# Audio tower on one core: the second group norm of the token stage one iteration behind the first, and the heads' weight products in three 16-bit passes

## What is computed

```python
# token stage, for each of 16 images
h = conv1d(x, conv_in_w, pad=3)                      # 64 -> 128 channels, 7 taps, 2048 positions
h = gelu(groupnorm1(h, gn1_w, gn1_b))                # first norm
h = conv1d(h, dw_w, stride=2, pad=2, groups=H) + dw_b   # 5 taps, 1024 positions
h = gelu(groupnorm1(conv1d(h, pw_w), gn2_w, gn2_b))  # pointwise product, second norm
# attention stage, 32 heads, 128 tokens (channels) per image, width 1024
h = h + attention(layernorm(h))                      # latents of 384 and 128, rotary part of 64
# last stage: base product plus two of eight small experts
h = h + ffn(layernorm(h))
```

## Time and profile before

| | |
|---|---|
| median of 3 runs | 2040.95 us (2040.42 to 2043.39) |
| the profiled execution | 2044.69 us, its span 2042.9 us |
| TensorE busy | 1892.5 us, 93% of the span |
| VectorE busy | 1321.2 us, 65% |
| ScalarE busy | 773.2 us, 38% |
| GpSimd busy | 308.4 us, 15% |
| mean granted clock of TensorE | 0.969 of full |

### The profile page before, as it was taken

The page is one execution under the profiler, slowest core; times in us unless marked ns, Lnnn a source line. Parts: engine busy times, 40 slices in busy tenths (PEclk is TensorE's granted clock), DMA queues, the critical chain, the costliest instruction groups (busy, mean ns, idle before and its releaser), DMA issues. The chain is left out here.

```text
span 2042.9 us, 32412 instructions
## 1 busy us (share of the span) xinstructions
PE 1892.5 (93%) x11538; PEld 1029.6 (50%) x11538; DVE 1321.2 (65%) x2742; ACT 773.2 (38%) x2020; POOL 308.4 (15%) x596
## 2 busy tenths in 40 slices
PE   4898898559999999999999999999999999859999
PEld 2344444335555555555555555555555555425554
DVE  4678777436666666666666666666666666555554
ACT  3454554233333334433333433333343333332221
POOL 2376675300000000000000000000000000033332
PEclk9899999679999999999999999999999999979999
DMA  5244342332222322232222222223222222243332
GB/s 143 52 86 96 81 95 65 76 91 51 58 58 59 76 56 53 58 76 59 58 58 55 73 58 58 58 58 75 55 55 58 40 39 39 39 138 80 80 82 73
DMA packets 305609, 138.87 MB, mean 68 GB/s; under 512 B 295088, under 2 KB 295344, under 8 KB 303408
## 3 DMA queue, kind: packets, MB, share of 16 engines
q1 hardware_dynamic: 301136, 108.35, 24.8%
q10 hardware_dynamic: 4320, 28.51, 4.0%
HBM read 56.07 MB, written 8.39 MB: 32 GB/s over the span
## 5 line engine op out<-in xcount | busy, mean ns | idle before, releaser
L1031 PE MATMUL out_ps<-m_h,ot_h 128*128 128x512 f16 x1024 | 389.4, 380 | 1.7 <-DVE ot_l L835 1.7
L1032 PE MATMUL out_ps<-m_l,ot_h 128*128 128x512 f16 x1024 | 389.0, 380 | 0.0
L1033 PE MATMUL out_ps<-m_h,ot_l 128*128 128x512 f16 x1024 | 388.9, 380 | 0.0
L756 ACT ACTIVATE qp_h<-qp_ps 128x512 f16<-128x512 f32 x126 | 75.3, 597 | 492.6 <-PE qp_ps L966 492.6
L812 ACT ACTIVATE prob<-s_ps,nmx 128x128 f32<-128x128 f32 x512 | 181.3, 366 | 207.3 <-DVE nmx L905 207.3
L885 DVE SCALAR_TENSOR_TENSOR resid<-out_ps,resid 128x512 f32<-128x512 f32 x256 | 176.1, 688 | 97.1 <-PE out_ps L1033 97.1
L835 DVE SCALAR_TENSOR_TENSOR qp_l<-qp_ps,qp_h 128x512 f16<-128x512 f32 x126 | 87.2, 692 | 234.5 <-ACT qp_h L756 234.5
L1221 POOL MEMSET fpower<- 128x1 f32 x1 | 0.1, 99 | 1392.4 <-POOLq L674 1392.4
L966 PE MATMUL qp_ps<-lat,wp_h 128*128 128x512 f16 x756 | 205.6, 381 | 0.0
L1033 PEld LDWEIGHTS out_ps<-m_h,ot_l 128*128 128x128 f16 x1024 | 100.4, 98 | 121.6 <-issue 1.4
L1031 PEld LDWEIGHTS out_ps<-m_h,ot_h 128*128 128x128 f16 x1024 | 100.5, 98 | 110.5 <-DVE ot_l L835 2.7
(11 more groups left out here) (217 smaller groups left out, 3861.3 us busy)
## 6 DMA issues: line engine op xcount, KB each, us to landing
wide<-heads_in ACTq DMA_DIRECT2D x30, 928.0 KB, 4.7
wide<-x_in SPq DMA_DIRECT2D x30, 512.0 KB, 6.5
tower_out<-result SPq DMA_DIRECT2D x16, 512.0 KB, 2.6
stage<-wb_in SPq DMA_DIRECT2D x8, 512.0 KB, 8.3
resid<-wqk_in SPq DMA_DIRECT2D x1, 2304.0 KB, 11.6
zt<-z SPq DMA_TRANSPOSE x128, 2.4
turned<-halves SPq DMA_TRANSPOSE x128, 3.0
wide<-heads_in SPq DMA_DIRECT2D x2, 928.0 KB, 4.6
```

The lines of the kernel that those rows point to most:

```text
L756: act.activation(out, src, ACT.Copy, scale=scale).then_inc(done, 1)
L1031: pe.matmul(out_ps[hf][:, :], ot_h[:, h, :], m_h[:, at], start=h == 0, stop=False)
L1032: pe.matmul(out_ps[hf][:, :], ot_h[:, h, :], m_l[:, at], start=False, stop=False)
L1033: last = pe.matmul(out_ps[hf][:, :], ot_l[:, h, :], m_h[:, at], start=False, stop=h == HEADS - 1)
```

## The change

**Token stage.** HID, PROJ and TAIL come one iteration later (2, 3, 4 become 3, 4, 5); a step PW at lag 2 holds the pointwise product and its statistics, which were at the end of the iteration of the taps; LOW is folded into TAIL. The conv has two PSUM banks in place of three, the pointwise product two pairs in place of one, and the averages share the second bank of the conv. Tap 0 goes from VectorE to ScalarE. On each engine the order within an iteration is new. In the last iterations, without conv, `squares` moves behind the next image's `hid`.

**Attention stage.** The raw weights of heads 4 to 31 are split by ScalarE and VectorE into 16-bit halves, in three pieces, in slots 0 to 2 of a round, into the place of the second raw buffer. `split_products` makes each product of three 16-bit passes, one slot later than its piece. The next head is loaded in slot 3 in place of slot 0. The scales by which the products are split take account of the new factor.

```diff
-    AHEAD, MID, HID, PROJ, TAIL, LOW = -1, 1, 2, 3, 4, 5
+    AHEAD, MID, PW, HID, PROJ, TAIL = -1, 1, 2, 3, 4, 5
...
-        conv_ps = [pb("conv_ps0"), pb("conv_ps1"), pb("conv_ps2")]
-        stat_ps = pb("stat_ps")
-        pw_ps = [pb("pw_ps0"), pb("pw_ps1")]
+        conv_ps = [pb("conv_ps0"), pb("conv_ps1")]
+        pw_ps = [[pb(f"pw_ps{b}{hf}") for hf in range(2)] for b in range(2)]
...
+        stat_ps = conv_ps[1][:, 0:4]
...
         @block.scalar
...
                 if ok(0):
                     copy_y1(i, p, 0)
-                if ok(AHEAD):
-                    x_high(i - AHEAD)
-                if ok(0):
                     copy_y1(i, p, 1)
-                if ok(MID):
-                    act.wait_ge(gn_step, i * GN_STEPS)
-                    need(act, dw_step, (i - MID) * DW_TAPS, B * DW_TAPS)
-                    act.activation(g1[:, DW_PAD:DW_PAD + T], y1[1 - p][:, :], ACT.Gelu, bias=c12[:, 1:2],
-                                   scale=c12[:, 0:1]).then_inc(gelu1_done, 1)
-                if ok(0):
                     copy_y1(i, p, 2)
                 if ok(HID):
...
+                if ok(MID):
+                    b = i - MID
+                    act.wait_ge(gn_step, i * GN_STEPS)
+                    need(act, dw_step, b * DW_TAPS, B * DW_TAPS)
+                    act.activation(g1[:, DW_PAD:DW_PAD + T], y1[1 - p][:, :], ACT.Gelu, bias=c12[:, 1:2],
+                                   scale=c12[:, 0:1]).then_inc(gelu1_done, 1)
+                    act.wait_ge(gelu1_done, b + 1)
+                    need(act, pw_done, b * 2, 2 * B)
+                    act.activation(dw[:, :], g1[:, 0:2 * D:2], ACT.Identity, bias=params[:, 5:6],
+                                   scale=params[:, 0:1]).then_inc(dw_step, 1)
+                if ok(AHEAD):
+                    x_high(i - AHEAD)
                 if ok(0):
                     copy_y1(i, p, 3)
...
         @block.gpsimd
...
                 if ok(MID) or ok(HID):
                     group_norms(i)
-                if ok(AHEAD) and i >= 0:
-                    x_low(i - AHEAD)
                 if ok(TAIL):
                     latent_scales(i - TAIL)
                 if ok(HID):
                     layer_norm(i - HID)
+                if ok(AHEAD) and i >= 0:
+                    x_low(i - AHEAD)
...
         @block.tensor
...
-                need(pe, y1_copied, i * 4 + (c - 2), 4 * B)
+                need(pe, y1_copied, i * 4 + (c - 1), 4 * B)
+                if c == 1:
+                    need(pe, s_copied, i, LAST + HID)
...
+                if ok(PW):
+                    pointwise(i - PW)
                 if ok(0):
                     conv(i, p, 1)
                     conv(i, p, 2)
                     conv(i, p, 3)
                 if ok(PROJ):
                     project(i - PROJ)
-                if ok(MID):
-                    pointwise(i - MID)
...
+            def raw_high(h, n):
+                if n == 0:
+                    act.wait_ge(raw_loaded[0], (h - HEADS) * 16 + 48)
+                    act.wait_ge(prod_done, h * 3)
+                    if h == HEADS:
+                        act.wait_ge(wr_lo, HEADS)
+                high(split_h[:, PIECES[n]], keep["wide0"][:, PIECES[n]], RAW_S, raw_hi)
...
+                    if more and j < len(PIECES):
+                        dve.wait_ge(raw_hi, now.t * 3 + (j + 1))
+                        low(split_l[:, PIECES[j]], keep["wide0"][:, PIECES[j]], RAW_S, split_h[:, PIECES[j]], raw_lo)
                     if after:
                         query_low(after, j)
...
+            def split_products(h, part, bank, free):
+                pe.wait_ge(raw_lo, (h - HEADS) * 3 + (part + 1))
+                pe.wait_ge(prod_lo, free)
+                ways = ((split_h, split_h), (split_h, split_l), (split_l, split_h))
+                if part == 0:
+                    for k in range(QT):
+                        for n, (a, b) in enumerate(ways):
+                            last = pe.matmul(bank[:, k * P:(k + 1) * P], a[:, RAW_Q + k * P:RAW_Q + (k + 1) * P],
+                                             b[:, RAW_K:RAW_K + P], start=n == 0, stop=n == 2)
+                else:
+                    at = RAW_O + (part - 1) * CHUNK
+                    for n, (a, b) in enumerate(ways):
+                        last = pe.matmul(bank[:, :], a[:, RAW_V:RAW_V + P], b[:, at:at + CHUNK],
+                                         start=n == 0, stop=n == 2)
+                last.then_inc(prod_done, 1)
```

More of the change, by code:

```diff
@@ L202, in body @@
                     sp.dma_start_transpose(ht[:, :, :], hid2[:, :]).then_inc(hid_turned, 16)
-                if ok(LOW):
-                    b = i - LOW
+                if ok(-2) and i >= -1:
+                    sp.wait_ge(x_hi, i + 2)
+                    sp.wait_ge(x_lo, i + 2)
+                    load(i + 2, 0, XW, x_loaded)
+                if ok(TAIL):
+                    b = i - TAIL
                     sp.wait_ge(lat_lo, b * 2 + 2)
@@ L505, in body @@
                     stats1(i, p, 1)
-                if ok(MID):
-                    for k in range(DW_TAPS):
-                        tap(i - MID, k)
+                if ok(PW):
+                    b = i - PW
+                    for hf in range(2):
+                        dve.wait_ge(pw_done, b * 2 + (hf + 1))
+                        dve.bn_stats(bn2[:, hf, :], pw_ps[b % 2][hf][:, :]).then_inc(bn2_done, 1)
+                    wait_apart(dve, dve_passed, (bn2_done, b * 2 + 2), (stat_done, i))
+                    mean_and_square(st2_ready, b, st[:, 2:4], bn2[:, :, :])
                 if ok(HID):
@@ L519, in body @@
                     dve.bn_aggr(st3[:, :], bn3[:, :, :]).then_inc(bn3_step, 1)
[L520 to L523 removed]
                 if ok(0):
                     stats1(i, p, 2)
+                if ok(TAIL):
+                    dve.wait_ge(rms_step, (i - TAIL) * RMS_STEPS + RMS_STEPS)
+                    dve.reciprocal(rinv[:, :], nrm[:, :]).then_inc(rinv_done, 1)
+                if ok(MID):
+                    for k in range(1, DW_TAPS):
+                        tap(i - MID, k)
+                if ok(0):
                     stats1(i, p, 3)
@@ L801, in body @@
             def body(before, now, after, more):
-                if more and (not now.known or now.t + HEADS + 1 < NH):
-                    act.wait_ge(prod_done, now.t * 3 + 3 * HEADS)
-                    act.wait_ge(wr_lo, now.t + HEADS)
-                    load(now.t + HEADS + 1, 1 - now.parity)
                 for j in range(QUAD):
                     s = now.slot + j
+                    if j == QUAD - 1 and now.t + HEADS + 1 < NH:
+                        act.wait_ge(wr_lo, now.t + HEADS + 1)
+                        act.wait_ge(raw_lo, now.t * 3 + 3)
+                        load(now.t + HEADS + 1, 0)
                     act.wait_ge(max_step, s * 2 + 2)
@@ L823, in body @@
                     if more and j:
-                        prod_high(now.t + HEADS, now.parity, now.side * -1 + 1, now.place, j - 1, prod_ps, False)
+                        prod_high(now.t + HEADS, 0, now.side * -1 + 1, now.place, j - 1, prod_ps, False)
                     act.wait_ge(av_done, s + 1)
@@ L926, in body @@
                     if more and j:
-                        prod_low(now.t + HEADS, now.parity, now.side * -1 + 1, now.place, j - 1, prod_ps)
+                        prod_low(now.t + HEADS, 0, now.side * -1 + 1, now.place, j - 1, prod_ps, RAW_S ** -2)
                     dve.wait_ge(o_hi, s + 1)
@@ L1063, in body @@
                     if more and j:
-                        products(now.t + HEADS, now.parity, j - 1, prod_ps, (now.t + HEADS) * 3 + (j - 1))
+                        split_products(now.t + HEADS, j - 1, prod_ps, (now.t + HEADS) * 3 + (j - 1))
                     if before or j:
```

117 lines of the change are left out of this document (55 added, 62 removed).

## The result

| | before | changed |
|---|---|---|
| median | 2041.53 us (2040.42 to 2043.39, 4 runs) | 2080.34 us (2079.56 to 2081.6, 4 runs) |
| ratio | | 1.019, 95% interval 1.0172 to 1.0207 |
| profiled span | 2042.9 us | 2077.8 us |
| mean granted clock | 0.969 | 0.956 |

The kernel became slower by 38.8 us. The timeline of the changed kernel comes first, because both questions (how long is an iteration, and what ends it) are answered there. These are its rows, start and duration in us: the first Gelu of several iterations, one steady iteration from 188.67 on, and the end of the token stage.

A forecast was written before the change was run, and what follows sets the result against it. TensorE's own work bounds attention; a ring of waits through TensorE, VectorE, GpSimd and ScalarE bounds the token stage. Period +38.7, iteration 1 -3, drain +7, attention -16.8: +26 us on 2040.95, so 2067 us, range 2030 to 2082.

The forecast's parts named there:

- the lock with loss of clock: Token stage, likeliest case: two-SBUF-input VectorE taps exclude GpSimd's x_low, which follows them; clock falls; 2055 to 2080 us, chance 0.45.
- The period: Token stage, steady iteration: 23.0 us at full clock plus 1.6 for lost clock, 24.6 us against 21.45 before.
- the count's own marks: Steady token iteration, times after its statistics matmul: first Gelu ends 11.4, tap 0 12.65, taps 17.9, x_low 22.0 us.
- x_low no longer blocks the weights' split: -3: Token stage, iteration 1: x_low no longer holds up VectorE's subtraction of the weights, 3 us saved.
- The drain: End of token stage: second norm a turn later, last statistics matmul behind a projection; +7 us, bounds 0 to 12.
- the DMA issues that I had put at nothing: Token stage, SyncE: the moved issues go out about 7 us before the projection that follows them.
- Attention: Attention stage, 28 heads: three fp16 passes replace one fp32 pass, 0.60 us less per head, -16.8 us, added splits at nothing.
- rounds shorter by 0.6 us: Attention stage, sign to look for: each round 0.6 us shorter, with TensorE's waits as few as before.
- the lock, but no loss of clock: Rival, token stage: 12 periods at 23.0 us, full clock; 2048 us (2042 to 2055), chance 0.22.
- No lock in the new place: Rival, token stage: x_low and taps run side by side, period 19.4 us, total 2000 us; faster cases 0.17 in all.
- The splits' rival: Attention stage: splits not hidden, each of 84 late by half, +27 us, about 2095 us, chance 0.06.
- Two conv banks cost nothing: Token stage: two conv banks rather than three cost nothing, since the copies no longer stand behind Gelus.

The follow-up runs named there:

- the shifted load: Changed kernel with the DMA issue of the second head's weights moved two iterations later; 2080.9 us, ratio 1.0189.
- attention half alone: Token stage of the kernel before with the attention stage of the changed kernel; 2026.61 us, ratio 0.9926.
- token half alone: Token stage of the changed kernel with the attention stage of the kernel before; 2094.23 us, ratio 1.0256.
- the filler: Changed kernel with 20 extra 512-column matmuls ahead of conv chunk 0 in images 4 to 15, result overwritten; 2059.71 us, ratio 1.0087.
- freed taps: Changed kernel, from image 2 taps 1 to 4 each two 512-column compares with a PSUM input instead of adding to dw, results not the tower's; 2023.91 us.
- e1: Changed kernel with x_high ahead of the copy of conv chunk 2 and x_low directly behind the group norm; 2038.64 us, ratio 0.9983.
- the drain mended: Better order plus two edits: second head's load two iterations later, last statistics matmul ahead of image 13's projection; 2016.78 us, ratio 0.988.
- the better order: Changed kernel with x_high behind chunk 0's copy, pointwise statistics ahead of chunk 1's, x_low between latents' scales and layer norm; 2021.53 us, ratio 0.9905.

## Why the prediction was right, and where it was not

The forecast was 2067 us, slower, by the lock with loss of clock; measured are 2080.34. In the steady iteration the mechanism is the predicted one at each place named. The size was missed by 13 us, +38.8 for +26, which is near the upper end of the range and just outside the 2055 to 2080 of the likeliest case. Every term of the sum erred to the same side. (In the count two marks are 0.1 us low by their own addends, the Gelu's 11.5 and tap 0's 12.7; nothing hangs on it.)

- *The period.* 24.6 was forecast, 24.7 is measured, and its parts by the experiments are 22.8 and 1.9 for 23.0 and 1.6. By the count's own marks, from the Gelu of iteration 2 to that of iteration 16, it is 341.0 us where it was 300.4, so +40.6 for 38.7. (Up to the copy of iteration 16, where the drain's term begins, it is +39.2; so the sum below doesn't count a stretch twice.) The marks hold too: layer norm ending with the taps, square-and-add 3.01 us, TensorE waiting 4.53. Tap 0 on ScalarE takes 1.32 us, not 1.24.
- *Iteration 1.* "x_low no longer blocks the weights' split: -3" was the wrong sign. The first Gelu did come 3.5 us earlier (38.38 for 41.85), and the split takes 1.36 us. But without a layer norm in front of it, x_low is issued while the second tap runs, and gets in before the third: the four taps last 8.94 us. The second Gelu is 1.5 us late instead of 3 early. So this term missed by 4.5 us. The count's 23.4 for iteration 2 was 25.3, with taps of 8.69 us. That iteration 15 gave this back, 17.9 (Gelus at 386.74 and 404.68) for 20.4, is luck.
- *The drain.* +7 was forecast, +10.4 measured, within the bounds. The step named (the last statistics matmul behind a projection) is there, and measured 3.4 us at the end. What the sum lacked is the wait that the projection itself has: the DMA issues that I had put at nothing stood behind the load of the second head, 2 us of it by the shifted load. The rest of these waits is not the load's: the kernel before, too, waits up to 9.0 us for a transpose in its last iterations, 24.3 us in three, where the changed kernel has 25.4 in four, one turn more.
- *Attention.* -16.8 was forecast, as 0.60 us in each of 28 rounds. The pair of traces gives 15.6, the run of it alone 14.5, but the rounds got only 0.40 us shorter (from the scores of one round to those of the next, 536.36 to 578.46 before and 583.52 to 625.22 now). That is 11.2 us in 28. The products are as costed: a 512-column one holds TensorE for 0.65 us (a product at 613.12, the next matmul at 613.77), the nine small ones for 0.50. What had no term is their cover. Once a round the scores follow the low half of the query (`qp_l`), and the last product stands between the two on TensorE:

```profile
536.08 0.38 PE L1073 MATMUL av_ps<-turned,kc 128*128 128x512 f16 x1
536.36 0.23 PE L1009 MATMUL s_ps<-lat,qp_h 128*128 128x128 f16 x1
```

```profile
582.77 0.69 DVE L856 SCALAR_TENSOR_TENSOR qp_l<-qp_ps,qp_h 128x512 f16<-128x512 f32 x1 [1.88 <-ACT qp_h L767]
583.02 0.38 PE L1113 MATMUL av_ps<-turned,kc 128*128 128x512 f16 x1
583.52 0.23 PE L1049 MATMUL s_ps<-lat,qp_h 128*128 128x128 f16 x1
```

  Before, the scores followed the last `av_ps` matmul by 0.28 us, now by 0.50: the product is 0.21 us shorter, but `qp_l` (to 583.46) comes no sooner behind the query, and TensorE stands idle for 0.12 us, in each of the 28 rounds. This is what is missing in the 498.56 of 500 us above. The added splits are not in the way, since VectorE was idle for 1.88 us before `qp_l`. That the stage still gained 15.6 is in part luck: at its start TensorE's wait for the first transposed `zt` fell from 5.56 to 3.76 us, which the sum didn't have. It is 3.77 with the attention half alone and 6.19 with the token half alone, so it comes with the attention half; that the load of the next head, moved out of the first slot, does it is likely and not shown. The forecast mark "rounds shorter by 0.6 us" did not hold.
- *The rest,* 3.9 us, is the difference between medians and profiled executions. Half of it may lie in attention: the kernel with the token half alone runs the attention stage of before, and takes 1372.1 us from its first `wp_l` to its last `ot_l` (473.95 to 1846.09) where before's own trace has 1374.2. Against that the changed stage is 13.5 us shorter. The remainder no trace assigns.

Of the rivals, "the lock, but no loss of clock" is what the filler made: 2059.7 where 2048 was put, with the missed terms in it. "No lock in the new place" had 19.4 us a period, and freed taps run at 19.8. The splits' rival fell with the attention half alone. Two conv banks cost nothing, as put: between 60 and 395 us TensorE never waits for a chunk's copy.

## What to carry to other kernels

Where two engines share a lock, an order is judged by what runs under the long instruction: put it beside work of the engines outside the lock, and look who waits there next, since moving it once put another instruction behind it (e1). Here the deeper pipeline bought nothing until that was done; then the kernel was 63.6 us faster than at the first attempt (2080.34 to 2016.78 us, with the drain mended). A step that gets shorter also covers less of what runs beside it: ask who waits behind it before counting its gain as a whole. And the drain and the first iterations lack some of the steady iteration's steps, so lay out each of them as a schedule of its own.

## What the hardware showed that I had not expected

- A waiting GpSimd instruction gets in between two back-to-back taps: x_low, issued at 43.79 in a run of four taps, stretched one of them to 4.98 us. I had counted such a run as one block.
- The lock is gone once one of the two inputs comes from PSUM: eight 512-column instructions (5.74 us) and x_low (3.82 us) run side by side.
- Tap 0, with one SBUF input, took 2.17 us beside x_low before and takes 0.80 us out of its way, so an instruction with one SBUF input can lose time beside x_low too. (The prediction put it under the rule for two inputs.) The Trainium skill's page "SBUF — State Buffer", section "Who interferes with whom", names `tensor_scalar` among those that can use the shared ports in a faster mode; both durations agree with it. In the changed order, with x_low elsewhere, tap 0 was the cheapest tap to leave on VectorE.
- A wait of 4.29 us and one of 4.53 us, an iteration apart, each left the granted clock at 0.50 behind them (178 to 181 us, 202 to 205). Waits of 0.88 and 1.43 us ahead of the pair, in the better order, left it at 1.00 (178 to 198 us), one of 1.80 us at 0.58 (154 to 157). But in the kernel before a wait of 2.24 us left the pair of 222.99 at its 1.98 us, and one of 2.23 us that of 266.01 at 3.45. So the length of the wait alone does not tell.
